# Forming the second mixer's matrix within the routing front instead of behind the expert slots

## The chip, the core and the metric

The kernel runs on one core of a Trainium2 chip. The metric is the device time of one execution in microseconds (us). Its engines are TensorE (PE, whose weight loads are listed as PEld), VectorE (DVE), ScalarE (ACT), GpSimd (POOL) and SyncE (SP, which here only issues transfers). Data lie in an on-chip memory of 128 partitions; TensorE writes to eight banks of 128x512 numbers. Every engine works through its own list of instructions in order, and the lists meet only in semaphores.

## What is computed

Two layers on x of 4 sequences (batches) by 512 tokens by 512 columns, each an adaptively scaled LayerNorm before a mixer and before a feed-forward part:

```
h = layernorm(x) * (1 + ca) + sa;  x = x + ga * linear_attention(h)    # 32 heads of 64
h = layernorm(x) * (1 + cb) + sb;  x = x + gb * mixture(h)             # 8 experts, 2 per token
h = layernorm(x) * (1 + ca) + sa;  x = x + ga * tuple_mixer(h)         # the second mixer
h = layernorm(x) * (1 + cb) + sb;  x = x + gb * sparse_ffn(h)          # 2 of 4 columns kept
```

The second mixer starts from a state of zeros, so it is linear up to a norm:

```
xi = (x @ W_in.T).reshape(b, l, NC, D)[..., None]
y = jnp.sum(C_real * nr - C_imag * ni, axis=-1)      # nr = B_real * xi, ni = B_imag * xi
out = y.reshape(b, l, NC * D) @ W_out.T
return x + _rmsnorm(out, norm_w)
```

So `out` is h times one 512x512 matrix M = W_in.T diag(k) W_out.T, where k sums C_real B_real - C_imag B_imag. The kernel forms M itself.

## The kernel before, in words

Every engine walks through the same stages, in the order that `walk` sets: a prologue, stage A (attention: 8 groups of heads, in each the 4 batches), the front, the slots, the back, stage C (the second mixer) and stage D (the sparse feed-forward). The order inside a stage is written out by hand, engine by engine.

A matrix product of full precision is mostly made of three passes over a high and a low part (`mm3`, lines 750 to 752), each part an fp32r tile; `hT` holds the normalised rows, transposed, its high half first and its low half behind it (8192 columns each). Stage A reads both halves. In its last step and in the front, `hF`, which lies over the high half alone, takes the transposed rows of the second LayerNorm for the router; the low half lies idle from the last projection on.

The **front** routes tokens, batch by batch. PE: `router(b)` (32 small products by `gwr`), `rows_back(b)` (16 transposes that bring the rows back into token order), `ln_transposes`, the last attention tail `tail_a`, and `prefix(b)` (counts tokens per expert). Between them stand ACT (copies out of the banks, the exponential) and VectorE (logits, choice, positions). POOL then scatters each batch's rows to DRAM by expert (`scatter`, eight indirect transfers a batch, line 2342). After the last batch VectorE writes the table of slots (`slot_table`).

The **slots**: 39 slots of 128 rows of one expert. For a slot ACT loads the rows (`hg`), PE transposes them (line 1019) and multiplies (`gate_up`, `down`), VectorE weights the result (`yt`, line 1996) by a gate that POOL has gathered (`gbt`, line 2403), and POOL adds it to `u_d` in DRAM (line 2417), one add after the other. SP loads an expert's weights, 3 MB into one of two buffers (`WB`), once the expert two before it is done (`load_expert`, line 615). Behind expert 2 SP also loads the eight sources of M (line 691, 512 KB each) into `mst`, which lies above the other slot tiles, and behind expert 3 two pieces of stage D's weights.

The **back**: on PE the 32 products that form M (line 1088; each shows as two records), plain fp32 and 128x512 columns, then the transposes of the third LayerNorm of batch 0 (line 781). ACT makes 16 gate diagonals, copies M's high part out of the banks (line 1464, `M_`), scales the rows of batches 0 and 1 (`ln_scaled`, line 1481) and only then writes the transposed rows (`ln_out`, lines 1239 and 1243). VectorE makes the diagonals' low parts, the LayerNorm statistics (lines 2030 to 2055) and M's low part (line 2062). Stage C begins with the first product by M (line 1114).

## Time and profile before

| | us |
|---|---|
| median of 3 executions | 1942.14 (1941.52 to 1944.3) |
| profiled execution, whole | 1948.09 |
| its span | 1945.8 |
| PE busy | 1805.1 (93%) |
| DVE busy | 1181.3 (61%) |
| ACT busy | 755.4 (39%) |
| POOL busy | 688.3 (35%) |
| chain that ended last | PE 76%, DVE 11%, issue 6%, ACT 2%, DMA 2%, POOL 2% |

The stages on the trace's clock: stage A to about 945 us, the front to 1018, the slots to 1250, the back to 1282, stage C to about 1360, then stage D. "Busy" counts the time in which an engine runs an instruction; the chain of waits is followed back from the last instruction, so its shares say what the end waited for. PEclk is the granted clock of TensorE: 1.00 is 2.4 GHz and 0.50 is 1.2 GHz. "DMA" is the mean busy share of the 16 DMA engines.

### The profile page before, as it was taken

To read this page: it belongs to the slowest core of one execution; us is meant where nothing else is said; L and a number is where in the kernel's file an instruction comes from. 1 tells how busy PE (TensorE), PEld (TensorE's weight loads), DVE (VectorE), ACT (ScalarE), POOL (GpSimd) and SP (SyncE) were. 2 spreads that over 40 slices of the span, in tenths; PEclk is the share of its full clock that TensorE was granted. 3 is DMA by queue.
4 is the path that set the end of the run, shared out by engine and by line. 5 is a ranking of instruction groups with operands and counts; after the bars stand their busy time and mean duration, and the time that the engine had idled before them with its cause. 6 is when DMAs were issued, how large, how long until landed. Compare 5 with 4: busy or idle time off the path is not lost.

```text
span 1945.8 us, 25658 instructions
## 1 busy us (share of the span) xinstructions
PE 1805.1 (93%) x8308; PEld 1416.0 (73%) x8308; DVE 1181.3 (61%) x2152; ACT 755.4 (39%) x1465; POOL 688.3 (35%) x678
## 2 busy tenths in 40 slices
PE   8889999999999999997749798999799999999996
PEld 5556878888888888875637676668688787787784
DVE  4556667766666667676844343556647566575654
ACT  2434554555455554543522232356622213213120
POOL 1335221221122222111354555534535536345442
PEclk9999999999999999998859898999899999999998
DMA  6122453535353525520286999610001101001011
GB/s 244 47 102 66 138 155 104 170 87 191 108 195 98 193 77 179 162 76 27 87 288 191 313 268 262 138 73 18 28 28 49 32 7 54 27 5 54 6 54 43
DMA packets 99905, 216.33 MB, mean 111 GB/s; under 512 B 8456, under 2 KB 33048, under 8 KB 98288
## 3 DMA queue, kind: packets, MB, share of 16 engines
q1 hardware_dynamic: 77696, 166.60, 26.4%
q0 software_dynamic: 11520, 28.96, 6.3%
q10 hardware_dynamic: 10608, 19.74, 3.3%
q8 instruction: 45, 0.74, 0.2%
q14 instruction: 36, 0.29, 0.1%
HBM read 123.93 MB, written 91.35 MB: 111 GB/s over the span
## 4 chain that ended last, share of the span: by engine, by line
PE 76%; DVE 11%; issue 6%; ACT 2%; DMA 2%; POOL 2%; ACTq 0%; POOLq 0%; DVEq 0%; SPq 0%
PE bank L750 21%; PE bank L752 20%; PE bank L751 20%; PE bank L1114 2%; PE bank L991 2%; PE bank L854 2%; DVE hh L2172 2%; PE bank L937 2%; PE bank L1088 1%; DVE rr L1857 1%; PE bank L1019 1%; DMA u_d<-yt,sm 1%; DVE fl L2150 1%; PE bank L824 1%; PE bank L939 1%
## 5 line engine op out<-in xcount | busy, mean ns | idle before, releaser
L1857 DVE RECIPROCAL rr<-rr 128x256 f32<-128x256 f32 x128 | 218.7, 1730 | 0.0
L750 PE MATMUL bank<-hT,W1b 128*128 128x512 f32 x512 | 208.0, 406 | 7.5 <-DVE hh L2125 7.5
L750 PE MATMUL bank<-W1a,hT 128*128 128x512 f32 x512 | 209.9, 410 | 3.4 <-DVE hT L1769 3.4
L751 PE MATMUL bank<-hT,W1b 128*128 128x512 f32 x512 | 203.4, 397 | 0.0
L752 PE MATMUL bank<-hT,W1b 128*128 128x512 f32 x512 | 203.1, 397 | 0.0
L752 PE MATMUL bank<-W1a,hT 128*128 128x512 f32 x512 | 201.3, 393 | 0.0
L751 PE MATMUL bank<-W1a,hT 128*128 128x512 f32 x512 | 200.7, 392 | 0.0
L2258 POOL TENSOR_TENSOR x<-x,tmp 128x512 f32<-128x512 f32 x64 | 101.3, 1583 | 271.4 <-DVE tmp L1849 271.4
L2125 DVE TENSOR_TENSOR hh<-hh,bank 128x512 f32<-128x512 f32 x64 | 43.3, 686 | 198.0 <-PE bank L752 168.4
L1882 DVE SCALAR_TENSOR_TENSOR kt<-bank,kt 128x256 fp32r<-128x256 f32 x128 | 50.7, 396 | 161.7 <-ACT vt L1318 161.5
L2192 POOL TENSOR_TENSOR W<-stage,W 128x1024 fp32r<-128x1024 f32 x32 | 77.0, 2406 | 184.5 <-ACT W L1193 182.2
L1556 ACT ACTIVATE ad<-hh 128x512 fp32r<-128x512 f32 x64 | 40.2, 632 | 254.8 <-DVE hh L2172 254.8
L1317 ACT ACTIVATE kt<-bank 128x256 fp32r<-128x256 f32 x128 | 49.3, 385 | 226.1 <-PE bank L752 225.5
L750 PEld LDWEIGHTS bank<-W1a,hT 128*128 128x128 f32 x512 | 96.7, 189 | 36.5 <-issue 15.5
L750 PEld LDWEIGHTS bank<-hT,W1b 128*128 128x128 f32 x512 | 96.9, 189 | 30.7 <-DVE hh L2125 10.0
L752 PEld LDWEIGHTS bank<-hT,W1b 128*128 128x128 f32 x512 | 96.8, 189 | 23.1
L752 PEld LDWEIGHTS bank<-W1a,hT 128*128 128x128 f32 x512 | 96.8, 189 | 21.8
L751 PEld LDWEIGHTS bank<-hT,W1b 128*128 128x128 f32 x512 | 97.1, 190 | 19.8
L750 PE MATMUL bank<-W1b,ot 128*128 128x512 f32 x256 | 103.5, 404 | 8.3 <-DVE tmp L1846 6.8
L750 PE MATMUL bank<-W,ad 128*128 128x512 f32 x256 | 102.6, 401 | 9.0 <-DVE ad L2179 8.9
L751 PEld LDWEIGHTS bank<-W1a,hT 128*128 128x128 f32 x512 | 97.2, 190 | 17.1
L750 PE MATMUL bank<-hT,W1a 128*128 128x512 f32 x256 | 103.1, 403 | 2.4 <-DVE yn L2086 1.5
(272 smaller groups left out, 4486.1 us busy)
## 6 DMA issues: line engine op xcount, KB each, us to landing
hs_d<-bor SPq DMA_DIRECT2D x24, 1548.0 KB, 11.2
ws_d<-W SPq DMA_DIRECT2D x48, 512.0 KB, 6.1
WB<-ws_d SPq DMA_DIRECT2D x8, 3072.0 KB
stage<-wa SPq DMA_DIRECT2D x32, 512.0 KB, 5.3
stage<-wbe SPq DMA_DIRECT2D x24, 512.0 KB, 4.3
stage<-wdn SPq DMA_DIRECT2D x24, 512.0 KB, 3.9
mw<-wmod SPq DMA_DIRECT2D x10, 1024.0 KB, 4.8
hg<-hs_d ACTq DMA_DIRECT2D x39, 258.0 KB
```

The costliest lines, as they stand in the source:

```text
L750: pe.matmul(o, lhs(HI), rhs(HI), start=start, stop=False, **kw)
L751: pe.matmul(o, lhs(HI), rhs(LO), start=False, stop=False, **kw)
L752: return pe.matmul(o, lhs(LO), rhs(HI), start=False, stop=stop, **kw)
L854: last = pe.matmul(o[0:NB, :], scT[:, layer, c, :], w[:, c * H:(c + 1) * H], start=c == 0, stop=c == NC - 1)
L937: pe.matmul(o[:, 0:2 * VW], kt[:, t % 2, HI, cols], vt[:, t % 2, :, pair, :], start=t == 0, stop=False, skip_group_check=True)
L1317: act.activation(kt[:, t % 2, HI, :], bank[t % 2][:, 0:256], ACT.Relu)
L1556: act.activation(ad[:, r, HI, :], hh[:, r, :], ACT.Copy).then_inc(d_hi, 1)
L1857: dve.reciprocal(rr[:, pair, h], rr[:, pair, h]).then_inc(r_rec, 1)
L1882: dve.scalar_tensor_tensor(out=kt[:, t % 2, LO, :], in0=bank[t % 2][:, 0:256], scalar=0.0, in1=kt[:, t % 2, HI, :].bitcast(F32), op0=ALU.m ...
L2125: dve.tensor_tensor(hh[:, r, :], hh[:, r, :], bank[4 + r % 2][:, :], ALU.mult).then_inc(d_h, 1)
L2192: return pool.tensor_tensor(dst, src, hi.bitcast(F32), ALU.subtract)
L2258: pool.tensor_tensor(xt, xt, tmp[:, (key + t) % 2, :], ALU.add).then_inc(ring_done, 1)
```

## The change

M's sources are loaded earlier and M is formed earlier. `mst` moves from above the slot tiles to columns 8192 to 16383, the low half of `hT`. SP loads the four sources with even numbers once batches 0 and 1 of the last group are projected, and the four odd ones once all are; the eight loads behind expert 2 go. ACT scales the even ones in the last step of stage A and the odd ones in the front, no longer in slots 16 to 23. PE forms M in banks 4 to 7 in three pieces, 5, 11 and 16 products, within the front; ACT and VectorE copy it out where the slots begin, and PE's first transposes and products of the slots wait for these copies, since they use the same banks. In the back PE, ACT and VectorE lose their parts.

```diff
-                    a("mst", [P, 8, 1024]), a("tab", [1, 5, TABW], I32), a("sm", [P, NS, 4]))
+                    a("tab", [1, 5, TABW], I32), a("sm", [P, NS, 4]))
+        def over_lo(a):
+            return a("before_mst", [P, 8192]), a("mst", [P, 8, 1024])
...
+        MB = bank[4:8]
...  SP
+            def m_load(part):
+                sp.wait_ge(pj_full, 6 * (NB * (GA - 1) + (2, NB)[part]))
+                for i in range(part, 8, 2):
+                    sp.dma_start(mst[:, i, :], winout[i]).then_inc(m_loaded[part], 16)
...  step_a, last group
                     if b == 2:
+                        m_load(0)
                         load_x_again(2)
...
             def front():
+                m_load(1)
                 load_x_again(3)
...
             def slots():
                 load_expert(2)
-                for i in range(8):
-                    sp.dma_start(mst[:, i, :], winout[i]).then_inc(m_loaded, 16)
                 load_expert(3)
...  PE
+            def matrix_part(i, m, start=False, stop=False):
+                last = pe.matmul(MB[m][:, :], mst[:, i, m * P:(m + 1) * P], mst[:, i, 512:1024], start=start, stop=stop)
+                if stop:
+                    last.then_inc(m_full, 1)
+            def matrix_even(first, last):
+                for k in range(first, last):
+                    if k == 0:
+                        pe.wait_ge(n_out, 2 * NB * GA)
+                        pe.wait_ge(m_scaled, 4)
+                    matrix_part(2 * (k // NC), k % NC, start=k < NC)
+            def matrix_odd():
+                pe.wait_ge(m_scaled, 8)
+                for m in range(NC):
+                    for i in range(1, 8, 2):
+                        matrix_part(i, m, stop=i == 7)
             def front():
                 router(1)
-                rows_back(1)
+                for i in range(NT * NC):
+                    if i == 2 * NC:
+                        matrix_even(0, 5)
+                    rows_back_part(1, i)
...
                 rows_back(2)
+                matrix_even(5, 16)
                 ln_transposes((1, 3), 0)
...
                 prefix(3)
+                matrix_odd()
...  rows_transpose; act_transpose waits for 2, down(i) for 3 + i
+                else:
+                    pe.wait_ge(m_lo, 1)
...  back: the 32 products go
-                pe.wait_ge(m_scaled, 8)
...  ACT
+            def matrix_scale(part):
+                act.wait_ge(m_loaded[part], 16 * 4)
+                for i in range(part, 8, 2):
+                    act.activation(mst[:, i, 512:1024], mst[:, i, 512:1024], ACT.Copy, scale=kcoef[:, i:i + 1]) \
+                        .then_inc(m_scaled, 1)
+            def matrix_hi():
+                for m in range(NC):
+                    act.wait_ge(m_full, m + 1)
+                    act.activation(M[:, HI, m, :], MB[m][:, :], ACT.Copy).then_inc(m_hi, 1)
...  slots
                 for i in range(3):
                     rows_load(i)
+                matrix_hi()
                 rows_hi(0)
...  VectorE, end of the front
                 slot_table()
+                matrix_lo()
```

How the lists change, as the two programs are built. On PE, in the front, from batch 1's router on (`gwr,hF` is the router, `ident,hF` is `rows_back`, `ident,h` are the LayerNorm transposes, `W1b,ot` the attention tail). Before:

```order
L824 MATMUL bank<-gwr,hF 128x8 x16
L812 MATMUL bank<-ident,hF 128x128 x16
L781 MATMUL bank<-ident,h 128x128 x16
L750 MATMUL bank<-W1b,ot 128x512
L751 MATMUL bank<-W1b,ot 128x512
```

Now:

```order
L834 MATMUL bank<-gwr,hF 128x8 x16
L822 MATMUL bank<-ident,hF 128x128 x8
L1008 MATMUL bank<-mst 128x512 x5
L822 MATMUL bank<-ident,hF 128x128 x8
L791 MATMUL bank<-ident,h 128x128 x16
L760 MATMUL bank<-W1b,ot 128x512
L761 MATMUL bank<-W1b,ot 128x512
```

Five products of M stand in the middle of batch 1's `rows_back`; eleven more stand between batch 2's `rows_back` and batch 3's LayerNorm transposes, and sixteen behind the last `prefix`, ahead of the first slot's transposes.

On ACT, behind the slots (the last `at` copy, the first weight splits of stage D, the diagonals, then the rows of the LayerNorm). Before:

```order
L1420 ACTIVATE at<-bank 128x256
L1193 ACTIVATE W1a<-stage 128x1024 x2
L1459 ACTIVATE dg<-ident,gcol 128x128 x16
L1464 ACTIVATE M_<-bank 128x512 x2
L1481 ACTIVATE xw<-x,cst 128x512 x4
L1481 ACTIVATE xnb<-x,cst 128x512 x4
L1464 ACTIVATE M_<-bank 128x512 x2
L1239 ACTIVATE tmp<-bank,modc 128x512
```

Now:

```order
L1468 ACTIVATE at<-bank 128x256
L1225 ACTIVATE W1a<-stage 128x1024 x2
L1503 ACTIVATE dg<-ident,gcol 128x128 x16
L1520 ACTIVATE xw<-x,cst 128x512 x4
L1520 ACTIVATE xnb<-x,cst 128x512 x4
L1271 ACTIVATE tmp<-bank,modc 128x512
```

The two copies of M are gone; both scalings of rows still stand ahead of the first `tmp`.

## Rows read from the trace of the kernel before

**Rows 1.** The chain of waits around the end of the slots: start us, us, what.

```profile
1250.17 27.48 PE bank L1088 x64
...
1282.60 0.77 PE bank L1114
```

**Rows 2.** ACT's timeline behind the slots: start us, us, instruction, [idle before <- releaser].

```profile
1273.42 2.93 ACT L1481 ACTIVATE xnb<-x,cst 128x512 f32<-128x512 f32 x4 [3.44 <-DVE cst L2055]
1277.68 1.09 ACT L1464 ACTIVATE M_<-bank 128x512 fp32r<-128x512 f32 x2 [1.33 <-PE bank L1088]
1278.65 0.78 ACT L1239 ACTIVATE tmp<-bank,modc 128x512 f32<-128x512 f32 x1
```

**Rows 3.** VectorE's timeline of the same stretch.

```profile
1266.94 1.28 DVE L2062 TENSOR_TENSOR M_<-bank,M_ 128x512 fp32r<-128x512 f32 x2
1268.14 2.46 DVE L2030 BATCH_NORM_STATS2 st<-x 128x6 f32<-128x512 f32 x4
```

**Rows 4.** VectorE's timeline of the slots, operation `yt` alone.

```profile
1064.41 0.75 DVE L1996 SCALAR_TENSOR_TENSOR yt<-bank,sm,gbt 128x512 f32<-128x512 f32 x1 [0.56 <-PE bank L752]
...
1069.28 0.75 DVE L1996 SCALAR_TENSOR_TENSOR yt<-bank,sm,gbt 128x512 f32<-128x512 f32 x1 [0.56 <-PE bank L752]
...
1079.45 0.75 DVE L1996 SCALAR_TENSOR_TENSOR yt<-bank,sm,gbt 128x512 f32<-128x512 f32 x1 [5.88 <-DMA gbt<-mod_rows_d,sm]
...
1117.04 0.75 DVE L1996 SCALAR_TENSOR_TENSOR yt<-bank,sm,gbt 128x512 f32<-128x512 f32 x1 [0.56 <-PE bank L752]
...
1161.17 0.75 DVE L1996 SCALAR_TENSOR_TENSOR yt<-bank,sm,gbt 128x512 f32<-128x512 f32 x1 [1.72 <-DMA gbt<-mod_rows_d,sm]
```

**Rows 5.** SyncE's timeline of the slots.

```profile
1054.72 0.37 SPq L615 DMA_DIRECT2D WB<-ws_d  x1
1055.14 12.67 SPq L691 DMA_DIRECT2D mst<-winout  x8
1083.68 0.38 SPq L615 DMA_DIRECT2D WB<-ws_d  x1
...
1117.08 74.82 SPq L615 DMA_DIRECT2D WB<-ws_d  x4
```

**Rows 6.** The chain of waits in the slots.

```profile
1103.07 6.77 issue
...
1131.57 2.25 issue
```

**Rows 7.** Busy us by stretch: length, PE, PEld, DVE, ACT, POOL, PEclk, DMA, GB/s.

```profile
1060.00:1065.00 5.00, 5.00 (x26) 4.04 (x25) 2.56 (x7) 1.37 (x3) 2.34 (x4) 1.00 1.00 337
997.00:1000.00 3.00, 3.00 (x14) 2.71 (x15) 1.85 (x10) 1.17 (x3) 2.39 (x3) 0.50 1.01 382
1000.00:1003.00 3.00, 2.29 (x14) 1.82 (x14) 2.26 (x13) 0.86 (x2) 1.97 (x3) 0.73 1.06 351
1260.00:1270.00 10.00, 10.00 (x25) 4.44 (x24) 9.55 (x34) 4.01 (x6) 0.00 (x0) 1.00 1.01 360
```

**Rows 8.** TensorE's timeline in the front.

```profile
956.83 1.97 PE L812 MATMUL bank<-ident,hF 128*128 128x128 f32 x8 [4.68 <-issue]
...
985.03 4.04 PE L781 MATMUL bank<-ident,h 128*128 128x128 f32 x16 [8.74 <-issue]
...
990.85 6.97 PE L824 MATMUL bank<-gwr,hF 128*128 128x8 f32 x32
```

**Rows 9.** Timelines of POOL, ACT and TensorE where the slots begin.

```profile
1006.03 0.95 POOL L2342 DMA_INDIRECT hs_d<-h,pos  x1 [1.01 <-DVE pos L1714]
...
1018.70 2.52 ACTq L1428 DMA_DIRECT2D hg<-hs_d  x3
...
1024.17 0.79 PE L750 MATMUL bank<-WB,hts 128*128 x1 [1.51 <-DVE hts L1966]
```

**Rows 10.** The tile `mst` (min/median/max ns), and ACT's timeline in the front.

```profile
L1448 ACT ACTIVATE mst<-mst,kcoef x8: 722/726/727, 1122.2 to 1160.5; 128x512 f32<-128x512 f32 x8
...
974.49 1.09 ACT L1265 ACTIVATE h<-bank 128x512 f32<-128x512 f32 x2 [11.09 <-PE bank L812]
```

More of the change, by code:

```diff
@@ L289, in over_hT @@
                     a("pps", [P, 2, 256]), a("at", [P, 2, 2, 2, MT], F32R),
-                    a("mst", [P, 8, 1024]), a("tab", [1, 5, TABW], I32), a("sm", [P, NS, 4]))
-        (hT, hF, (hg, hts, sgs, pps, at, mst, tab, sm)) = shared(
-            [lambda a: a("hT", [P, 2, NC, NB * S], F32R), lambda a: a("hF", [P, NC, NB * S]), over_hT])
+                    a("tab", [1, 5, TABW], I32), a("sm", [P, NS, 4]))
+        def over_lo(a):
+            return a("before_mst", [P, 8192]), a("mst", [P, 8, 1024])
+        (hT, hF, (hg, hts, sgs, pps, at, tab, sm), (_, mst)) = shared(
+            [lambda a: a("hT", [P, 2, NC, NB * S], F32R), lambda a: a("hF", [P, NC, NB * S]), over_hT, over_lo])
         hold1 = sb("hold1", [P, 16384])
@@ L501, in build @@
         x_back = [sem(f"b_x_loaded{b}") for b in range(NB)]
-        m_loaded = sem("m_loaded")
+        m_loaded = [sem(f"m_loaded{i}") for i in range(2)]
         m_scaled = sem("m_scaled")
@@ L1048, in act_transpose @@
                     pe.wait_ge(at_lo, i)
+                else:
+                    pe.wait_ge(m_lo, 2)
                 for k in range(2):
@@ L1057, in down @@
                     pe.wait_ge(y_evac, i - 1)
+                else:
+                    pe.wait_ge(m_lo, 3 + i)
                 def w(s, k):
@@ L1080, in back @@
             def back():
-                pe.wait_ge(m_scaled, 8)
-                for half, banks in ((0, (0, 1)), (1, (4, 5))):
-                    if half == 0:
-                        pe.wait_ge(s_p, SLOTS)
-                    for ic in range(8):
-                        for j in range(2):
-                            m = 2 * half + j
-                            last = pe.matmul(bank[banks[j]][:, :], mst[:, ic, m * P:(m + 1) * P], mst[:, ic, 512:1024],
-                                             start=ic == 0, stop=ic == 7)
-                    last.then_inc(m_full, 1)
                 for half in range(2):
@@ L1369, in step_a @@
                 ins.then_inc(kvb_hi, 1)
+                if b == 3 and last:
+                    matrix_scale(0)
                 if not first:
@@ L1388, in front @@
                 ln_out((1, 2), 1)
+                matrix_scale(1)
                 rows_out(2, 0)
@@ L1444, in slots @@
                         rows_load(i + 4)
-                    if 16 <= i < 24:
-                        if i == 16:
-                            act.wait_ge(m_loaded, 16 * 8)
-                        act.activation(mst[:, i - 16, 512:1024], mst[:, i - 16, 512:1024], ACT.Copy,
-                                       scale=kcoef[:, i - 16:i - 15]).then_inc(m_scaled, 1)
                 act_hi(SLOTS - 1)
@@ L1460, in back @@
                             .then_inc(dg_hi, 1)
-                for half, banks in ((0, (0, 1)), (1, (4, 5))):
-                    act.wait_ge(m_full, half + 1)
-                    for j in range(2):
-                        act.activation(M[:, HI, 2 * half + j, :], bank[banks[j]][:, :], ACT.Copy).then_inc(m_hi, 1)
-                    if half == 0:
-                        ln_scaled(2, 0)
-                        ln_scaled(2, 1)
+                ln_scaled(2, 0)
+                ln_scaled(2, 1)
                 ln_out((2, 0), 0)
@@ L2056, in c_scales, with matrix_lo @@
                                              op0=ALU.mult, op1=ALU.mult).then_inc(c_scaled, len(lns))
-            def matrix_lo(half):
-                for j in range(2):
-                    m = 2 * half + j
+            def matrix_lo():
+                for m in range(NC):
                     dve.wait_ge(m_hi, m + 1)
-                    dve.tensor_tensor(M[:, LO, m, :], bank[((0, 1), (4, 5))[half][j]][:, :], M[:, HI, m, :].bitcast(F32),
+                    dve.tensor_tensor(M[:, LO, m, :], MB[m][:, :], M[:, HI, m, :].bitcast(F32),
                                       ALU.subtract).then_inc(m_lo, 1)
@@ L2068, in back @@
                 c_scales((2, 0))
-                matrix_lo(0)
                 c_stats(2, 1)
                 c_scales((2, 1))
-                matrix_lo(1)
             def gated(b, t):
```

## The prediction

> **What bounds the kernel now.** I read the chain of waits first: TensorE carries 76% of it, so an edit pays only where PE's stretch is on the chain and nothing else is close behind. Three places matter here, and each has another limit.
>
> Behind the slots, PE spends 27.48 us on the 32 products that form M, and stage C opens at 1282.60 [rows 1]. The obvious forecast is that these 27.5 us go. The timelines of ACT and VectorE beside them say otherwise: ACT scales batch 1's rows from 1273.42 to 1276.35, after waiting for VectorE's statistics, then copies M and starts the first `tmp` of the LayerNorm at 1278.65 [rows 2]. These statistics hang on the last slot's add, the load of x from DRAM and 16 diagonals, not on M. PE's work is covered by another chain almost as long.
>
> In the slots the beat is one `yt` every 4.87 us (1064.41 to 1069.28), while from 1069.28 to 1117.04 seven slots take 47.76 us instead of 34.09: 13.7 us are lost [rows 4]. The first loss ends with `yt` waiting 5.88 us for a gathered gate [rows 4]; in the second PE stands for 6.77 us, from 1103.07 to 1109.84, where expert 3 begins [rows 6]. SP's timeline shows the cause: expert 2's 3 MB go out at 1054.72, the eight sources of M from 1055.14 on (they take 12.67 us only to issue), expert 3 at 1083.68 [rows 5]. The DMA engines are full, 1.00 at 337 GB/s [rows 7].
>
> In the front PE is often idle: 4.68 us in batch 1's `rows_back` and 8.74 us ahead of batch 3's transposes, and behind the second gap 16 transposes take 4.04 us and the router 6.97 us [rows 8], with the granted clock at 0.50 as late as 997 to 1000 [rows 7].
>
> **The change part by part.**
>
> *Loads out of the slots.* Removed are 8 x 512 KB = 4.19 MB from a stretch with full DMA engines; at 337 GB/s [rows 7] that is 12.4 us. From the other side: expert 4, loaded with nothing ahead of it in SP's queue, is issued at 1117.08 [rows 5] and PE goes on at 1131.57 + 2.25 = 1133.82 [rows 6], 16.7 us later. Expert 3 took 1109.84 - 1083.68 = 26.2 us, 9.5 us more; what stood ahead of it was what was left of `mst`. PE gets to expert 3's first slot 1103.07 - 1083.68 = 19.4 us after the issue, four beats, so a load of 16.7 us is in time. What is late next: experts 4 to 7 wait for their own transfers as now (2.25 us of PE at expert 4), so nothing is given back there. The two 512 KB pieces of stage D's weights remain behind expert 3; at the pace of 3.15 MB in 16.7 us they take another 5.6, so the queue is empty 22.3 us after expert 3's issue, while expert 4's load is issued five beats, 24.3 us, after it (expert 2 has five slots). Gathers keep being slowed by an expert's load alone: `yt` waits 1.72 us at 1161.17 [rows 4]. I leave 1.4 us of the 13.7 for such waits: gain **12.3**, bounds 8 and 13.7, near the 12.4 from bytes.
>
> *The same loads in their new place.* The four even ones are issued before the attention tail of batch 0's last group, the four odd ones before `load_x_again(3)`, whose wait for batch 2's tail comes after the last projection that the odd loads wait for. 2.1 MB at 337 GB/s are 6 us, each time in a stretch of attention that loads little; the first scatter comes later. Behind them in SP's queue wait the reloads of x for batches 2 and 3, which POOL adds a whole step later, or which wait longer for a tail. Cost 0, bound 1 us.
>
> *Scaling.* Eight copies of 0.726 us on ACT leave the slots and come back as four and four; the second four stand before a wait of 11.09 us [rows 10], the first four where ACT waits for the tail. Cost 0; in the slots ACT was idle most of each beat, so their going gains 0 too.
>
> *Five products in `rows_back(1)`.* One is 27.48 / 32 = 0.859 us at the full clock [rows 1, 7]. Five are 4.3 us, and the gap is 4.68 us. At half clock they would be 8.6 us and push 3.9 us on. The eight transposes behind the gap (1.97 us [rows 8]) are faster if PE is kept at work. I take +0.3, bounds -0.7 and +3.9.
>
> *Eleven products ahead of batch 3's transposes.* 9.45 us into a gap of 8.74 us [rows 8]: +0.7. But PE then comes to the transposes at full clock. The chain there runs through transposes, the prefix, the router (6.97 us) and batch 3's prefix; POOL's last scatters wait for its result, at 1006.03 [rows 8, 9]. If the clock held throughout, half of the router's 6.97 and of the rest, at most 5 us, would go. The router's 128x8 products keep PE listed as busy with little work, and from 997 to 1000 the clock was still low with PE busy all the time [rows 7]. So I count on the clock for the transposes, the prefix and part of the router: -3.7, with the +0.7 a net **-3.0**, bounds -5 and +1.
>
> A rule speaks against this. The trace first: from 1000 to 1003 the mean granted clock rises to 0.73 from 0.50, behind a stretch in which PE did little but `rows_back` transposes [rows 7]. The Trainium skill ("TensorE: Matmul & The Clock Gate", Part 4: PE-mode transpose) holds that transposes don't count as PE work for the clock. By that rule the -3.7 would shrink towards nothing, since what follows M's products is transposes and the router; by the row transposes can count. I go by the row.
>
> *Sixteen products behind the last prefix.* 13.7 us at full clock, started near 1001 and over near 1015, while POOL still scatters. Then ACT issues the three row loads (2.52 us [rows 9]), copies four banks (1.09 us for two [rows 2]: 2.2), copies the first rows (0.6, by the same row), and VectorE's low part follows (0.7, half of the pair's 1.28 [rows 3]). With 0.15 of hand-over that is 6.2 us from the first row load to the first slot product, where now it is 1024.17 - 1018.70 = 5.5 [rows 9]. Cost **+0.7**, bounds 0 and +3 (if M's last products end after the loads, at a low clock). Behind the waiting `M_` copies on VectorE stands only the first slot's work.
>
> *The back.* PE's 27.48 us go. VectorE no longer does its first two low parts, so the statistics of batch 1 start at 1266.94 instead of 1268.14 [rows 3], 1.20 earlier. ACT's scaling of batch 1 then runs from 1272.22 to 1275.15, and `tmp`, next in its list, follows at once: 1275.15 instead of 1278.65, **-3.5**. PE now stands idle for some 20 us before, comes at 1.2 GHz and has two transposes of four still ahead of it: +0.2. Net -3.3, bounds -4 and -2.5. So 24 of the 27.5 us in the back are not gained.
>
> Sum: -12.3 + 0 + 0.3 - 3.0 + 0.7 - 3.3 = **-17.6 us**. The sum is made against a profiled execution of 1948.09 us (span 1945.8), which would become 1930.5; the median of the plain runs is 1942.14, 5.95 less, and becomes **1924.5**.
>
> **The rivals.**
>
> *A. Gathers stay slow (0.13).* Only the wait for expert 3 goes. The loss at 1079.45, where `yt` waited 5.88 us [rows 4], stays because expert 2's own load fills the DMA engines. For it: the u_d adds and gathers form a chain that lags more with each slot once DMA is full. Against it: `yt` waited only 1.72 us under expert 5's load [rows 4]. Slots then give 7.8: 1929. 
>
> *C. The whole 27.5 us leave the back (0.03).* It needs x's statistics to have waited for M. Against it: ACT waited for VectorE [rows 2], VectorE for nothing of PE. It gives 1942 - 27.5 - 12.3 - 2.0 = 1900.
>
> *D. Slower (0.05): M's products run at 1.2 GHz in the front.* They take 1.72 us each there. Five end 3.9 us late; eleven take 18.9 us in a gap of 8.7, +10.2; sixteen take 27.5 us behind a prefix that is by then 14 us late, and end some 11 us after the rows have come. The front gets 25 us longer, less 12.3 and 3.3: 1951.5. It decides from about 16 us of delay in the front on. For it: the front's clock is 0.50 in long stretches [rows 7]. Against: these same products ran at 1.00 for as long as they lasted (1260 to 1270 [rows 7]).
>
> **How the numbers follow.** My forecast has 0.68. It is 1924.5 with an own range of 1919 to 1931 from the bounds (slots +-3, front +-3, not all at one end). The range 1917 to 1934 takes in A and B and leaves C and D out. What a measurement of this kernel can tell from no change is about 0.2%, 3.9 us. Faster by more than that: the forecast, A, B and C less 0.01, 0.94; slower: 0.04 of D's 0.05; within: what is left of both, 0.02.
>
> **What would show it.** In the profile after: no `yt` interval over 6 us at experts 2 and 3, and PE not idle at expert 3's start; the later stops at experts 4, 6 and 7 unchanged. DMA full for about 17 us after expert 2's load, then less. In the front, M's products at some 0.86 us each (two records), the last scatters of POOL starting about 3 us earlier, first slot product 6.2 us after the first row load. In the back PE idle for about 20 us, first `tmp` 25.0 us after the last slot product instead of 28.5 (1278.65 - 1250.17). The sum is wrong if expert 3 still takes over 20 us to come, if the products in the front take 1.7 us each, or if stage C opens over 8 us sooner behind the slots than the 32.4 us of now (1282.60 - 1250.17).

## The result and the profile after

The changed kernel takes 1936.13 us (median of 7 runs, 1933.12 to 1939.7), the kernel before beside it 1941.52 (7 runs). The ratio is 0.9972, 95% interval 0.9959 to 0.9986: 5.4 us faster, with 2.7 to 8.0 in the interval, and so just over the 0.2% that I had named as what a measurement can tell. On two further chips the ratio was 0.9983 [0.9971, 0.9996] and 0.9977 [0.9965, 0.9989], 12 runs each. The mean of the three is 4.4 us. I had forecast 17.6 us and a time of 1924.5; 1936.1 lies outside the range.

The profiled execution took 1938.58 us (span 1936.2). First the page's head, then TensorE's timeline in the front (start us, us, instruction, idle before); it answers to [rows 8, 9].

```profile
span 1936.2 us, 25661 instructions
PE 1803.2 (93%) x8308; PEld 1411.5 (73%) x8308; DVE 1181.4 (61%) x2152; ACT 754.3 (39%) x1465; POOL 687.9 (36%) x678
```

```profile
953.01 5.36 PE L1008 MATMUL bank<-mst 128*128 128x512 f32 x10
...
977.28 9.61 PE L1008 MATMUL bank<-mst 128*128 128x512 f32 x22
986.73 1.04 PE L791 MATMUL bank<-ident,h 128*128 128x128 f32 x8
...
991.31 6.07 PE L834 MATMUL bank<-gwr,hF 128*128 128x8 f32 x32
...
1003.89 16.72 PE L1008 MATMUL bank<-mst 128*128 128x512 f32 x32
1023.23 1.09 PE L1057 MATMUL bank<-ident,hg 128*128 128x128 f32 x4 [2.61 <-DVE M_ L2101]
1025.83 0.79 PE L760 MATMUL bank<-WB,hts 128*128 x1 [1.51 <-DVE hts L2006]
```

The 5 and 11 products sit in the gaps that they were meant for. The sixteen behind the last prefix took 16.72 us, not 13.7, and ended at 1020.61, about a microsecond before the last of the three row loads was out, so that nothing waited for them. The first transposes behind the eleven run at full speed (8 in 1.04 us where 16 took 4.04 [rows 8]), but the router behind them takes 6.07 us, against 6.97. The windows (length, PE, PEld, DVE, ACT, POOL, PEclk, DMA, GB/s) say why: the clock falls while that router runs.

```profile
990.00:992.00 2.00, 2.00 (x20) 2.00 (x19) 0.37 (x3) 1.26 (x2) 0.09 (x1) 1.00 1.05 383
992.00:994.00 2.00, 2.00 (x13) 2.00 (x13) 0.83 (x5) 0.00 (x0) 0.79 (x1) 0.59 1.03 404
994.00:997.00 3.00, 3.00 (x15) 3.00 (x16) 0.00 (x0) 0.00 (x0) 2.09 (x3) 0.50 0.93 305
```

Where the slots begin, ACT issues the rows, copies M, and VectorE follows; the first slot product comes 6.62 us behind the first row load, where it was 5.47 [rows 9].

```profile
1019.21 2.51 ACTq L1476 DMA_DIRECT2D hg<-hs_d  x3
1021.76 2.07 ACT L1333 ACTIVATE M_<-bank 128x512 fp32r<-128x512 f32 x4 [17.94 <-issue]
1022.39 2.48 DVE L2101 TENSOR_TENSOR M_<-bank,M_ 128x512 fp32r<-128x512 f32 x4 [10.37 <-ACT M_ L1333]
```

In the slots, SyncE's timeline and VectorE's (`yt` alone, one per slot), answering to [rows 4, 5]:

```profile
1056.37 24.70 SPq L625 DMA_DIRECT2D WB<-ws_d  x2
1081.12 7.97 SPq L553 DMA_DIRECT2D stage<-wdn  x2
1109.46 29.58 SPq L625 DMA_DIRECT2D WB<-ws_d  x2
```

```profile
1076.29 0.75 DVE L2036 SCALAR_TENSOR_TENSOR yt<-bank,sm,gbt 128x512 f32<-128x512 f32 x1 [1.06 <-DMA gbt<-mod_rows_d,sm]
1081.00 0.75 DVE L2036 SCALAR_TENSOR_TENSOR yt<-bank,sm,gbt 128x512 f32<-128x512 f32 x1 [0.90 <-DMA gbt<-mod_rows_d,sm]
1090.54 0.75 DVE L2036 SCALAR_TENSOR_TENSOR yt<-bank,sm,gbt 128x512 f32<-128x512 f32 x1 [5.57 <-DMA gbt<-mod_rows_d,sm]
...
1125.42 0.75 DVE L2036 SCALAR_TENSOR_TENSOR yt<-bank,sm,gbt 128x512 f32<-128x512 f32 x1 [1.61 <-DMA gbt<-mod_rows_d,sm]
1138.61 0.75 DVE L2036 SCALAR_TENSOR_TENSOR yt<-bank,sm,gbt 128x512 f32<-128x512 f32 x1 [0.56 <-PE bank L762]
```

The reader is to see three things. There is still one long wait for a gathered gate, 5.57 us, where it was 5.88 [rows 4], but it stands elsewhere: before, at the ninth `yt`, 24.7 us behind the issue of expert 2's load, with `mst` in SP's queue; now the ninth waits 1.06 us (1076.29), and it is the eleventh that waits, at 1090.54, with expert 3's load issued at 1080.70 (the second of the first two `WB` rows). Near 1100 to 1110 the longest interval is 6.20 us, where it was 11.10. But one at 1125.42 is long: 13.19 us between two `yt`, 8.3 more than a beat, where expert 4 begins. The chain of waits has it as PE standing 7.17 us, where it stood 2.25 before [rows 6]:

```profile
1124.35 7.17 issue
```

From the first `yt` to the last it is 208.3 us after, 215.0 before. Behind the slots (ACT, VectorE, PE; [rows 1 to 3]):

```profile
1267.20 2.93 ACT L1520 ACTIVATE xnb<-x,cst 128x512 f32<-128x512 f32 x4 [2.24 <-DVE cst L2095]
1270.04 0.76 ACT L1271 ACTIVATE tmp<-bank,modc 128x512 f32<-128x512 f32 x1
```

```profile
1273.96 0.76 PE L1146 MATMUL bank<-M_,hT 128*128 128x512 f32 x1 [0.66 <-ACT tmp L1271]
```

`tmp` follows batch 1's scaling at once. Last `yt` to stage C's first product is 28.8 us, in place of 32.4.

### The profile page after: what moved, and what is told of

It is laid out like the page before. It is cut to its first block, busy times and chain, and to the rows that moved or that the text cites. A ratio compares the mean times of both kernels' runs of the same rounds, so it can differ in the third digit from the quotient of the medians.

```text
span 1936.2 us, 25661 instructions
## 1 busy us (share of the span) xinstructions
PE 1803.2 (93%) x8308; PEld 1411.5 (73%) x8308; DVE 1181.4 (61%) x2152; ACT 754.3 (39%) x1465; POOL 687.9 (36%) x678
## 4 chain that ended last, share of the span: by engine, by line
PE 75%; DVE 12%; issue 6%; ACT 3%; DMA 2%; POOL 2%; ACTq 0%; POOLq 0%; DVEq 0%; SPq 0%
PE bank L760 21%; PE bank L762 20%; PE bank L761 20%; PE bank L1001 2%; PE bank L1146 2%; PE bank L864 2%; DVE hh L2209 2%; PE bank L947 2%; DVE rr L1896 1%; DMA u_d<-yt,sm 1%; PE bank L1008 1%; PE bank L1057 1%; DVE fl L2187 1%; PE bank L949 1%; DVE tmp L1888 1%
## 5 line engine op out<-in xcount | busy, mean ns | idle before, releaser
L760 PE MATMUL bank<-hT,W1b 128*128 128x512 f32 x512 | 208.0, 406 | 7.5 <-DVE hh L2162 7.5
```

Source lines behind the costliest of these rows:

```text
L760: pe.matmul(o, lhs(HI), rhs(HI), start=start, stop=False, **kw)
```

## The experiments

Two accounts had to be told apart. **Theory 1** is my forecast: each byte loaded behind expert 2 costs its time at the full rate, and nothing is given back. The other says that the slots' pace comes from the experts' own loads and the gathers, so that only what still waits in SP's queue when expert 3's load is issued costs anything (**theory G**; theory 2 in the first expectations), against a cost in proportion to the bytes (**theory P**). Theory 3 is about the front's clock, theory 4 about the one profile that I had read. All ratios are to the kernel before, on the same chip.

**Before and after once more** (no edit), for the spread of what a profile shows.

> The kernel before, once more, for a second profile. Theory 1: the time lost in the slots between expert 2's and expert 3's loads is again near 13.7 us, in the stall at expert 3. Theory 4 (the profile of before on which the sum was made was an unlucky execution): it is 5 to 9 us, the whole slot phase is 3 to 5 us shorter than 215.0 us, and the span is nearer 1940 than 1946 us.

> The changed kernel, once more, for a second profile. If the stall of 8.3 us at expert 4 is a property of the kernel, it is there again within 2 us and the slots take 208 us; if it wanders from execution to execution, the slots' length stays near 208 while the long intervals stand at other experts.

> The changed kernel, timed beside the two that follow, as the dose of nothing. All theories: 1936 us within 2 us, ratio to before 0.997.

> The changed kernel, beside the other three: 1936 us within 2 us, ratio to before 0.9978 within 0.001; slots 206 to 210 us.

> A third profile of the kernel before. Its slots took 215.0 and 208.9 us in the first two, expert 3's load 26 us in both. Theory G lets the source loads cost what of them still waits when expert 3's load is issued, which varies: slots of 208 to 216 us, the mean of the three 3 to 6 us over the mean without source loads there (207.7 us over eight profiles).

Times 1942.4, 1936.12, 1937.59 (median of 12), 1937.51 (12), 1940.2. The table sets all profiles of this study side by side that bear on the slots. The idle columns are what PE's timeline shows ahead of the first product of expert 3 and of expert 4 (- is under 1.3 us), slots is first to last `yt`, and load 3 is from issue to landing where the profile has it.

| kernel | MB behind expert 2 | load 3 | PE idle at 3 | at 4 | slots |
|---|---|---|---|---|---|
| before, 1st | 4.19 | | 6.77 | 2.25 | 215.0 |
| before, 2nd | 4.19 | 25.8 | 4.74 | 2.14 | 208.9 |
| before, 3rd | 4.19 | | 4.55 | 3.18 | 211.9 |
| after, 1st | 0 | | - | 7.17 | 208.3 |
| after, 2nd (e4) | 0 | 20.5 | - | 7.80 | 210.5 |
| after, 3rd (e12) | 0 | 20.3 | - | 3.25 | 206.2 |
| after, 4th (e12b) | 0 | | - | 4.82 | 212.4 |
| loads only (e1) | 0 | 20.9 | - | 2.26 | 205.1 |
| loads only (e1b) | 0 | | - | 3.54 | 207.5 |
| half again (e7) | 2.10 | | - | 1.73 | 208.3 |
| loads again (e2) | 4.19 | 27.8 | 7.79 | 3.70 | 216.6 |
| loads again (e2b) | 4.19 | 21.9 | - | 3.60 | 209.4 |
| twice again (e6) | 8.39 | 28.8 | 18.89 | - | 225.8 |
| late slices (e3) | 0 | | - | 3.73 | 207.2 |
| no eleven (e8) | 0 | | - | 4.68 | 208.2 |
| shorter ends (e10) | 0 | | - | 4.08 | 209.0 |
| milder form (e11) | 0 | 19.4 | - | 2.78 | 206.9 |
| milder form (e11b) | 0 | | - | 5.71 | 206.9 |

The three profiles of before have 211.9 us of slots in the mean, the eleven without source loads behind expert 2 have 208.0.

The next table takes the slots apart: microseconds lost against a beat of 4.87, between `yt` of given numbers (the loads of experts 3 and 4 are issued behind the tenth and the fifteenth slot).

| kernel | 1st to 10th | to 15th | to 21st | to the last |
|---|---|---|---|---|
| before (3), mean | 4.8 | 8.4 | 4.3 | 9.5 |
| each | 4.6, 5.0, 4.7 | 9.1, 7.8, 8.3 | 4.0, 3.9, 5.0 | 12.3, 7.2, 8.8 |
| after (4), mean | 2.8 | 3.8 | 8.7 | 9.1 |
| each | 0.3, 3.9, 1.1, 5.8 | 4.1, 3.9, 3.4, 3.8 | 9.7, 10.7, 6.6, 7.7 | 9.2, 7.0, 10.1, 10.2 |
| loads only (2) | 0.0, 0.2 | 4.4, 3.8 | 5.9, 5.8 | 9.8, 12.8 |

My profile of before had the longest slots and the longest idle at expert 3 of its three. But the loss that I had priced, 13.7 us from the eighth `yt` to the fifteenth, is 12.3 and 13.1 us in the other two; what made that execution's slots long lies behind the twenty-first. So theory 4, an unlucky execution, does not hold for the term of the sum. Of the 13.7 us, 5.3 came at the gathers (1069.28 to 1079.45 less a beat of 4.87 [rows 4]) and the other 8.4 up to expert 3. The stall at expert 4 is there in all four profiles of the changed kernel; its longest `yt` interval was 8.3 us over a beat in the first and 8.2, 5.1 and 6.5 in the others.

**The loads alone** (e1, e1b).

```diff
 loads of mst and their scaling: as changed
-  matrix_even(0, 5); matrix_even(5, 16); matrix_odd()    # PE front
-  matrix_hi() / matrix_lo()                              # where the slots begin
+  the 32 products, copies and low parts in the back, as before
```

> The eight source loads and their scalings stand in the front as in the changed kernel; the 32 products and the copies of M stay in the back as in the kernel before. Theory 1 (the loads cost the slots the forecast 12.3 us): the slots take 12.3 us less than before's in every execution, the back is as before, the front unchanged: 12 us under before in the timed runs, about 1930 us. Theory 2 (an expert's load slows the gathers and their adding DMAs whatever is queued behind it, and the stall moves to expert 4): the slots gain only 2 to 7 us, so 1935 to 1940 us, and the single add under expert 2's load takes about 8.4 us here too. Theory 3 (the early products give the front 3 us by the clock): this kernel starts its slots later than the changed kernel by 2 to 3 us; if they give nothing, its first row load comes at the same time within 1 us.

> Loads and scalings of the sources early, the 32 products and the copies of M in the back, as run once before. Beside the changed kernel on one chip. By the profiles so far the products' move takes 3.5 us out of the back, gives back 1.2 us at the slots' start and 0.7 us behind the back, and is worth 1 us (4 of 7) to 2.5 us in the front by the clock: this kernel is 2.5 to 4 us slower than the changed one (1939 to 1941 us). If the slots' pace, set by the experts' loads, takes up what is won in front of them, it is level within 1 us.

Measured 1937.73 us (0.9976 [0.9959, 0.9993]) and 1937.71 (0.9974 [0.9962, 0.9985]); on the second chip the changed kernel had 0.9977. So the loads give the whole gain, 4.9 us, and the products' move nothing that could be measured, against 2.5 to 4 expected. Theory 1 wanted 1930. Its profiles have the back at 32.4 us, unchanged, and a front 1.5 us longer than the changed kernel's mean (73.8 and 74.2 us against 72.5), less than the 2 to 3 us of theory 3 and more than the 1 us that would have ruled it out.

**The loads once more, in three doses** (e7: four, e2 and e2b: eight, e6: sixteen).

```diff
   load_expert(2)
+  sp.wait_ge(m_full, 4)
+  for i in range(4 | 8 | 16):
+      # with 16, the second load of a row waits for its first
+      sp.dma_start(mst[:, i % 8, :], winout[i % 8]).then_inc(m_again, 16)
   load_expert(3)
```

> As the kernel that loads the eight sources a second time behind expert 2, but with four of them (2.10 MB). With eight, 2.86 MB of the 4.19 had moved in the profile of before when expert 3's load was issued, and the timed runs put the whole at 5.6 us over the changed kernel. Theory G (what still waits in SP's queue when expert 3's load is issued is all that counts; the rest fills a time in which the DMA engines would have idled): nothing is left over, expert 3's load takes 20 to 21 us from issue to landing as in the changed kernel, and the time is within 1.5 us of the changed kernel's, 1936 to 1938 us. Theory P (every byte costs its share of 5.6 us): 2.8 us over it, 1939 us, and expert 3's load takes 23 to 24 us. Theory 1 (forecast, each byte at the full rate): 6.2 us, 1942 us.

> The changed kernel, with the eight source loads (4.19 MB) issued a second time behind expert 2, into the same rows, which nobody reads again; everything else is in place. Only the slots can differ from the changed kernel's. Theory 1 (forecast): +12.3 us against the changed kernel, 1948 us, with the long interval at expert 3. Theory 2: the transfers cost what the medians of before and after leave beside the back's 3.5 us, that is 2 to 3 us, 1938 to 1940 us, and the single add under expert 2's load keeps its 8.4 us; the stall at expert 4 is shorter than in the changed kernel (4 instead of 8 to 9 us).

> The eight source loads a second time behind expert 2 (4.19 MB), as run once before. Theory G (only what still waits in SP's queue when expert 3's load is issued counts) and theory P (every byte its share): 4 to 7 us over the changed kernel, expert 3's load near 27 us from issue to landing. Theory 1 (forecast, each byte at the full rate): 12 us over it.

> The eight source loads a second and a third time behind expert 2 (8.39 MB), each row's last load behind the landing of the one before it, all ahead of expert 3's load. Theory G: the idle share of the DMA engines is used up by the first 4.19 MB, and the next moves at the full 337 GB/s: 12.4 us more than with eight, 17 to 19 us over the changed kernel, 1954 us. Theory P: twice the cost of eight, 11 us, 1947 us. Theory 1: 25 us, 1961 us.

Measured: four 1939.55 us (0.9978 [0.9964, 0.9992]); eight 1941.77 (1.0001 [0.9984, 1.0018]) and 1940.01 (0.9993 [0.9980, 1.0006]); sixteen 1953.77 (1.0075 [1.0062, 1.0089]). Against the mean of the changed kernel's three ratios, 0.9977, that is 0.1, 3.8 (mean of two) and 19.0 us. Beside the changed kernel on the one chip where all three were timed (0.9983), eight cost 1.9 and sixteen 17.9 us. The cost is not in proportion: the second dose of 4.19 MB cost 15 to 16 us where the first cost 2 to 5. (The half dose alone, 0.1 against theory P's 2.8, would not have decided it, with an interval of 2.7 us to each side.) Theory P (11 us for sixteen) and theory 1 (25) fail, theory G (17 to 19) holds. Two of its details don't: one profile with eight had expert 3's load at 21.9 us in place of 27, with no idle PE (SP's queue had carried 6.69 MB between the two issues there and 5.85 in the other, so that 0.65 and 1.49 MB were left), and the second dose cost a little more than 12.4, which the intervals don't tell apart from it. The load of expert 3 in the profiles of the 2nd before, the 2nd after, e2, e2b and e6, one line each (last column us from issue to landing):

```profile
WB<-ws_d SPq DMA_DIRECT2D x1, 3072.0 KB, 25.8
```

```profile
WB<-ws_d SPq DMA_DIRECT2D x1, 3072.0 KB, 20.5
```

```profile
WB<-ws_d SPq DMA_DIRECT2D x1, 3072.0 KB, 27.8
```

```profile
WB<-ws_d SPq DMA_DIRECT2D x1, 3072.0 KB, 21.9
```

```profile
WB<-ws_d SPq DMA_DIRECT2D x1, 3072.0 KB, 28.8
```

And e6's PE ahead of expert 3, the stall that 8.39 MB make:

```profile
1122.26 0.79 PE L766 MATMUL bank<-WB,hts 128*128 x1 [18.89 <-issue]
```

Expert 3's load is hardly longer than with eight, 28.8 against 27.8 us, and yet PE stands 11 us longer. That is because of how the dose is given: each second load waits on SP for its first, so that SP issued the sixteen until 1092.56 and expert 3 only then. The tenth `yt`, about when it is issued otherwise, was at 1083.82 (SP's timeline of e6):

```profile
1055.08 37.48 SPq L707 DMA_DIRECT2D mst<-winout  x16
1093.24 0.38 SPq L626 DMA_DIRECT2D WB<-ws_d  x1
```

So what costs in e6 is all that was still to be moved at 1083.8, 5.3 MB, part of it not yet issued. What the first 4.19 MB displaced stands in the DMA queues between the issue of expert 2's load and of expert 3's (queue: packets, MB, share of 16 engines' time). Before, 1054.7 to 1083.7, mean 332 GB/s:

```profile
q1 hardware_dynamic: 2330, 6.01, 55.0%
q0 software_dynamic: 976, 2.26, 33.0%
q10 hardware_dynamic: 720, 1.32, 14.3%
```

After, 1056.4 to 1081.1, mean 269 GB/s:

```profile
q0 software_dynamic: 919, 2.14, 41.8%
q1 hardware_dynamic: 1552, 3.15, 34.7%
q10 hardware_dynamic: 720, 1.32, 16.4%
```

SP's queue (q1) carried 6.01 MB before, 3.15 of them expert 2's weights: 2.86 of `mst`'s 4.19 MB were through before expert 3's load was issued. Only the other 1.33 MB stood in front of expert 3. The rest used a time that the transfers after don't ask for: expert 2's load is through at 1073.3, and until expert 3's issue SP's queue is empty (length, PE, PEld, DVE, ACT, POOL, PEclk, DMA, GB/s):

```profile
1056.40:1073.30 16.90, 16.90 (x87) 13.73 (x86) 8.38 (x20) 4.79 (x11) 7.38 (x12) 1.00 1.01 315
1073.30:1080.70 7.40, 7.40 (x37) 5.98 (x36) 3.67 (x10) 2.04 (x5) 5.33 (x10) 1.00 0.72 173
```

The gathers show the same from POOL's side (us from issue to landing, last column). In the second profile of before, one issued under expert 2's load with `mst` behind it, then three beside `mst` alone:

```profile
gbt<-mod_rows_d,sm POOLq DMA_INDIRECT x1, 7.4
gbt<-mod_rows_d,sm POOLq DMA_INDIRECT x3, 8.9
```

In the third of the changed kernel, one under expert 2's load, two with SP's queue all but empty, three under expert 3's load:

```profile
gbt<-mod_rows_d,sm POOLq DMA_INDIRECT x1, 8.1
gbt<-mod_rows_d,sm POOLq DMA_INDIRECT x2, 4.4
gbt<-mod_rows_d,sm POOLq DMA_INDIRECT x3, 9.7
```

So `mst` did slow the gathers once expert 2's load was through; without it the slow ones are those under expert 3's load.

**Late slices** (e3): the other neighbour of expert 3's load.

```diff
   load_expert(3)
-  wd_slice(0, 0)
-  wd_slice(0, 1)
   for e in range(4, GE):
       load_expert(e)
+  wd_slice(0, 0)
+  wd_slice(0, 1)
```

> The changed kernel, with the two 512 KB slices of wdn issued behind the last expert's load in place of behind expert 3's. If expert 3's load takes 20.5 us, against 16.5 to 18 us of the others, because the slices share the DMA engines with it or because of their backlog at expert 4, it falls by 2 to 3 us and expert 4's from 22.6 to 18 us: 3 to 6 us less than the changed kernel, 1930 to 1933 us. If expert 4's stall comes from the gathers and adds alone, both stay and the time is 1936 us within 1 us.

1936.96 us, 0.9968 [0.9953, 0.9982], slots 207.2 us, PE idle 3.73 at expert 4. This is level with the changed kernel within the intervals. The profile lacks the load's landing; in e11, which has this edit too, expert 3's load took 19.4 us, so the slices make at most about 1 us of what lies between 20 and 16.7.

**Without the eleven products** (e8).

```diff
   rows_back(2)
-  matrix_even(5, 16)
   ln_transposes((1, 3), 0)
```

> The changed kernel without the eleven products ahead of batch 3's transposes; M lacks these eleven terms. The time from the end of the last head's products to the first row load was 73.6, 74.6 and 73.8 us in the profiles without early products and 73.1, 71.2 and 72.5 us with them. If the eleven products raise the clock for the last router, as forecast, this goes back to 74 us, and the kernel is 1 to 2 us slower than the changed one. If they only fill an idle time, it stays at 72 to 73 us or falls by the 0.7 us that they delay batch 3's transposes, and the kernel is 0 to 1 us faster.

M lacks these eleven terms here. 1940.55 us, 0.9989 [0.9976, 1.0003]: 2 to 3 us slower than the changed kernel, though with less work. On the same chip the three kernels that keep the eleven products had 0.9968 (e3), 0.9974 (e10) and 0.9978 (e7). The time to the first row load was 74.05 us; it is counted, in the expectation too, from where the last head's products start. Its front reads as the one before, half speed from the transposes on:

```profile
986.38 4.04 PE L791 MATMUL bank<-ident,h 128*128 128x128 f32 x16 [8.76 <-issue]
...
992.20 6.97 PE L834 MATMUL bank<-gwr,hF 128*128 128x8 f32 x32
```

In the third profile of the changed kernel the same router, with the eleven products ahead, took 4.46 us:

```profile
973.86 9.61 PE L1008 MATMUL bank<-mst 128*128 128x512 f32 x22
983.30 1.04 PE L791 MATMUL bank<-ident,h 128*128 128x128 f32 x8
...
987.13 4.46 PE L834 MATMUL bank<-gwr,hF 128*128 128x8 f32 x32
```

So the eleven products do raise the clock for what follows, and how far into the router it lasts differs: 6.07 us or 4.46 in the profiles of one kernel. That they cost less than they bring is what the times point to; the intervals overlap.

**Shorter ends** (e10), and a milder form with the late slices (e11, e11b).

```diff
   e11, e11b: the wdn slices late, as in e3
-  for i in range(3): rows_load(i)
-  matrix_hi(); rows_hi(0); rows_load(3)
+  rows_load(0); matrix_hi(); rows_load(1); rows_hi(0); rows_load(2); rows_load(3)
   ...  ACT, back
-  ln_scaled(2, 0); ln_scaled(2, 1); ln_out((2, 0), 0); ln_out((2, 0), 1)
+  ln_scaled(2, 0); ln_out((2, 0), 0); ln_out((2, 0), 1); ln_scaled(2, 1)    # e10
+  ln_scaled(2, 0); ln_out((2, 0), 0); ln_scaled(2, 1); ln_out((2, 0), 1)    # e11
   ...  VectorE, back; e10 alone:
-  diagonals(all); c_stats(2, 0); ...
+  diagonals(batch 0); c_stats(2, 0); ...; diagonals(batches 1 to 3)
```

> The changed kernel with three moves. The copies of M stand between the first row load and the second, in place of behind the third: the first slot's product 1.3 us earlier (5.3 in place of 6.6 us behind the first row load). In the back VectorE forms only batch 0's diagonals ahead of the statistics, and the other twelve behind them: the statistics start when the rows are there, 2.4 us earlier. ScalarE writes out batch 0's transposed rows ahead of batch 1's scaling: another 3.5 us. If VectorE's statistics and the order on ScalarE bound the back, as the forecast said, the back is 22 to 24 us in place of 28.8 us and the kernel is 6 us under the changed one, 1930 us; if the load of the rows or something else bounds it, 0 to 2 us.

> The changed kernel with the wdn slices behind the last expert's load (0 to 1 us by its own run), the copies of M between the first and the second row load (slot start 1.2 us earlier, as its profile showed), and in the back the order half 0 of batch 0, scaling of batch 1, half 1 of batch 0. With batch 1's scaling last, the first product came 3.7 us earlier and 2.5 us of it were lost waiting for batch 1's rows; with it in the middle the first product is 2 to 3 us earlier and that wait is under 1 us. Sum 3 to 5 us under the changed kernel, 1931 to 1933 us. If what is won at the slots' start is taken up by the experts' loads, which set the slots' pace, 1 to 2 us.

> The changed kernel with the late wdn slices, the copies of M between the row loads, and batch 1's scaling between the halves of batch 0, as run once before: again 2 to 4 us under the changed kernel if that was no chance.

e10: 1938.81 us, 0.9974 [0.9962, 0.9986], no gain over the changed kernel; 6 us expected. The start of the slots did come (5.48 us from row load to first product), and stage C's first product stood 25.1 us behind the last `yt`. But VectorE's statistics began no earlier, since x itself is late, and PE then waited for batch 1's rows (VectorE's timeline of e10, then TensorE's):

```profile
1258.23 2.47 DVE L2071 BATCH_NORM_STATS2 st<-x 128x6 f32<-128x512 f32 x4 [3.17 <-DMA x<-u_d]
```

```profile
1271.73 0.77 PE L1146 MATMUL bank<-M_,hT 128*128 128x512 f32 x1 [0.74 <-ACT tmp L1271]
...
1276.34 0.69 PE L805 MATMUL bank<-ident,xnb 128*128 128x128 f32 x2 [2.46 <-ACT xnb L1521]
```

e11 took 1931.92 us (8 runs; 0.9968 [0.9953, 0.9983]) where the changed kernel had 0.9983, and e11b 1934.03 (5 runs; 0.9959 [0.9944, 0.9975]) where it had 0.9977: 2.9 and 3.5 us less, twice in the same direction with intervals that overlap. It is the best of the versions run, some 7 us under before. Its stage C opens 27.8 and 27.7 us behind the last `yt`, against 28.8 to 29.3.

## Why the prediction was wrong, point by point

The profiles of before (three) against those of the changed kernel (four), as means in us, beside the terms of the sum:

| stretch | forecast | before | after | difference |
|---|---|---|---|---|
| start of the last head's products to first row load | -2.7 | 74.0 | 72.5 | -1.5 |
| to the first slot product | +0.7 | 5.5 | 6.6 | +1.2 |
| first to last `yt` | -12.3 | 211.9 | 209.4 | -2.6 |
| to stage C's first product | -3.3 | 32.4 | 28.9 | -3.5 |
| the rest behind it | 0 | 661.2 | 661.7 | +0.5 |

With +0.15 from the first slot product to the first `yt`, that is -5.7 us; the timed ratios say 4.4.

- **The step that failed: the slots' -12.3.** It took the loss up to the fifteenth `yt` from 13.7 to 1.4 us and gave nothing back behind it. Measured as means, that loss went from 13.2 to 6.6, and 4.4 us came back from the fifteenth to the twenty-first. Three of its steps fell.
  - (a) The 4.19 MB were priced at 337 GB/s, as though something waited behind every byte. But most of `mst` went through in a time in which SP's queue stands empty without it (1073.3 to 1080.7, 173 GB/s); the doses put the first 4.19 MB at 2 to 5 us and the next at 15 to 16.
  - (b) I put expert 3's 26.2 us against expert 4's 16.7, and 1.4 us for slow gathers. Expert 3's load takes 20.3 to 20.9 us with nothing ahead; my own test, wrong if over 20 us, is met. It no longer stops PE (under 1.3 us idle in place of 6.77, 4.74 and 4.55, 5.4 in the mean), so the mechanism of the removed wait is right. But gathers slowed by this load cost 3.4 to 4.1 us in the same stretch. With them PE gets to expert 3 only 20.4 to 23.8 us after the issue, where I had 19.4.
  - (c) "Nothing is given back" at experts 4 to 7: PE's idle time at expert 4 is 7.17, 7.80, 3.25 and 4.82 us after, 2.25, 2.14 and 3.18 before, +3.2 us in the mean. Expert 4's load took 22.6 and 19.6 us in two profiles after, 16.5 in the second of before. The queues beside it suggest why (first profiles): 2.05 MB of gathers and adds in the 22.0 us after, 1.24 MB in the 16.7 us before, when PE's stop at expert 3 had just thinned them out. From its issue until PE goes on, expert 4's load takes 18.1 to 22.8 us in the thirteen profiles without a stop at expert 3, and 16.6 to 18.2 in four of the five with one (in the fifth, e6, PE doesn't stop at expert 4). That this traffic is the cause was not tested by itself, and it does not set the size: e1, with the same loads and no stop at expert 3 either, has 2.26 and 3.54 us of idle PE at expert 4, hardly more than before.
- **One profile was taken for the kernel.** Its 215.0 us of slots stand 3.1 over the mean of three, but little of that was in the sum: the 13.7 us were 13.0 in the mean.
- **Rival A** (0.13, 1929) is borne out in its size and not in its place. It kept the loss at the ninth `yt` because of expert 2's own load. In the first profile that interval fell from 10.17 us to 5.36 without `mst`, while a like one came up under expert 3's load (9.54). It is not always so: in two of the four profiles of the changed kernel 3.9 and 5.8 us are still lost up to the tenth `yt`. By the page "DMA: Bandwidth & Descriptors" of the Trainium skill (Queues, rings and completion order) a gather's delay should depend on SP having something queued and not on how much; the trace agrees (the gather issued under expert 2's load lands after 7.4 us with `mst` behind it and after 7.9, 8.1 and 7.2 without, and the next one after 8.9 us with `mst` and 5.1, 4.1 and 4.4 with SP's queue all but empty). **Rival B** (0.11, 1933) is borne out in part, 20 us in place of 16.7, though not by the stage D weights. Slow gathers and a long load, with what expert 4 takes back, make the time; I had priced each alone and given 0.24 to the two.
- **The back, -3.3**: right, -3.5. The edits behind it held too: of PE's 27.5 us only what ACT's chain let through was gained. **Rival C** is out.
- **The front, -2.7**: -1.5. The eleven products raise the clock, as e8 shows, but it falls again inside the router, at 992 in the first profile. I had counted 3.7 us; from the router's start to the last prefix it is 11.33 to 11.36 us in the six profiles without the eleven products, and 10.43, 8.88, 8.81 and 9.99 with them (8.8 to 10.4 in all twelve). Over these twelve the time to the first row load is 71.2 to 74.4 us, 72.9 in the mean, against 74.0 without, so the front's gain may be nearer 1.1. The Trainium skill ("TensorE: Matmul & The Clock Gate", Part 4: PE-mode transpose), which I weighed and set aside, would let the clock fall while only transposes run. The clock fell behind transposes, prefix and part of the router, so the rule is not contradicted, and no run here tells transposes from the router's small products. **Rival D** is out as a price: M's products took 0.87 us each (9.61 / 11) in the second gap. But they were not at full speed everywhere: the five took 5.36 us (4.3 in the sum), at a granted clock of 0.83, and the sixteen 16.72 (13.7), at 0.55 up to 1010; both found room.
- **The slots' start, +0.7**: +1.2. The path is another than I had it. PE's transposes of the first rows wait for VectorE's first low part (1023.23, 2.61 idle), so that behind the row loads (2.51) stand ACT's first copy, the low part, the transposes (1.09), and only then the copy and the low part of the rows; I had all four copies in a line and left the transposes out. e10 took this term away by its order (5.48).
- **The products' move** was worth -5.3 in the sum and nothing in the times (e1 against the changed kernel). The profiles do show the back's 3.5 us. The slots are where they may go: 209.4 us in the mean of four with the move, 206.3 in the two profiles of e1, with 2.7 us of the difference up to the tenth `yt` and 2.9 at expert 4, less 2.2 behind it. The ranges of the slots overlap, and what would couple them is not known; this stays open.

## What to carry to other kernels

A wait that a transfer ends is not worth its bytes at the full rate. It is worth about what of the queue still stands ahead when the awaited load could be issued, and that is read from the bytes moved between the two issues, with and without the load; a doubled load tells whether the rate has room left, if it does not itself hold back the next issue. A wait that is gone can leave another one behind it, here of gathers under the next load, so the stretch is to be priced as a whole. In a chain of loads of which each is issued by the progress of the work, the next one's margin under full traffic has to be in the sum: here it took back 4.4 us in the changed kernel and 1.5 in e1. And a phase whose length wanders by 6 us from profile to profile needs more than one profile, taken apart by stretch, before its loss is priced.

## What the hardware showed that I had not expected

The software queue's transfers (gathers and adding writes) took more of the DMA engines' time per byte than SP's loads here: after, 1109.5 to 1131.5, they took 42.1% for 2.05 MB where 3.15 MB of weights took 38.8%, that is 4.5 against 2.7 us of all 16 engines for each MB (42.1% and 38.8% of 22.0 us).

```profile
q0 software_dynamic: 877, 2.05, 42.1%
q1 hardware_dynamic: 1552, 3.15, 38.8%
```

So the busy share alone says little of what there is room for. Between the issues of expert 2's and 3's loads the three queues' shares add up to 92.9% after and 102.3% before, 9 points apart, while the rates, 269 and 332 GB/s, are 23% apart. Further, the same instructions at the same place ran at another clock in two profiles of one kernel (the router 6.07 and 4.46 us).
